# Attention kernel on one core: the key matmuls of the pair after next moved behind the second scores

## What is computed

```
q = rmsnorm(layernorm(x) @ Wq, gq)      # per head, D = 128, 16 heads
k = rmsnorm(ctx @ Wk, gk);  v = ctx @ Wv
scores = einsum('bqhd,bkhd->bhqk', q, k) / sqrt(D)
x = x + (softmax(scores) @ v) @ Wo
h = square(relu(layernorm(x) @ ternary(W_fc).T))
x = x + rmsnorm(h) @ ternary(W_proj).T
```

## Time and profile before

| | |
|---|---|
| runs | 370.31, 370.45, 375.02 us; median 370.45 us |
| span of the profiled execution | 373.6 us (its own device time is not listed apart; the span is 3.15 us over the median of the runs) |
| TensorE clock granted, mean | 0.981 of full speed; 1.00 from 40 to 340 us |
| busy | PE 347.3, DVE 308.3, ACT 295.5, POOL 256.4 us |

### The profile page before, as it was taken

How to read it: one execution, slowest core, us unless ns; L and a number is a source line. 1 busy time by engine, 2 the same in 40 slices (tenths; PEclk the granted TensorE clock), 3 DMA queues, 4 the chain that set the end, 5 groups by cost and what they waited for, 6 DMA issues and landing times.

```text
span 373.6 us, 9069 instructions
## 1 busy us (share of the span) xinstructions
PE 347.3 (93%) x2720; PEld 330.7 (89%) x2720; DVE 308.3 (83%) x697; ACT 295.5 (79%) x810; POOL 256.4 (69%) x386
## 2 busy tenths in 40 slices
PE   6778999999999999999999999999999999888975
PEld 5768999999999999999999999999999998767865
DVE  2797788888888888888888898888888986799991
ACT  3447888888888888888888888888888888777750
POOL 3653777777777787777777877777778773065761
PEclk9989999999999999999999999999999999999995
DMA  6980111111111111111111111111111100000012
GB/s 212 366 281 6 55 42 42 42 42 42 44 44 42 42 42 45 42 42 44 42 44 43 42 43 42 44 42 44 45 51 53 51 1 0 2 0 2 0 38 75
DMA packets 20341, 20.72 MB, mean 55 GB/s; under 512 B 1504, under 2 KB 19936, under 8 KB 20192
## 3 DMA queue, kind: packets, MB, share of 16 engines
q1 hardware_dynamic: 20032, 20.45, 16.9%
q10 hardware_dynamic: 288, 0.00, 0.0%
HBM read 19.40 MB, written 1.05 MB: 55 GB/s over the span
## 4 chain that ended last, share of the span: by engine, by line
PE 48%; DVE 17%; POOL 13%; issue 12%; DMA 4%; ACT 3%; POOLq 1%; SPq 0%; DVEq 0%; ACTq 0%
POOL fq L297 7%; PE bY L547 6%; DVE WWl L869 4%; PE bT L585 4%; PE bY L549 4%; PE bY L548 4%; PE bA L547 3%; PE bA L548 3%; PE bA L549 3%; PE bT L595 3%; POOL Wkh L274 3%; DVE Ol L869 3%; DMA Wkr<-in_L_xattn_Wk 3%; PE bO L547 2%; PE bO L549 2%
## 5 line engine op out<-in xcount | busy, mean ns | idle before, releaser
L416 ACT ACTIVATE Pr<-bS,nb,fq 128x256 f32<-128x256 f32 x128 | 70.9, 564 | 1.7 <-DVE nb L918 1.7
L411 ACT ACTIVATE Oh<-bO 128x256 fp32r<-128x256 f32 x64 | 24.6, 385 | 29.5 <-PE bO L549 29.1
L277 POOL TENSOR_TENSOR Wql<-Wqr,Wqh 128x512 fp32r<-128x512 f32 x32 | 41.4, 1293 | 5.9 <-POOL Wqh L274 5.9
L914 DVE TENSOR_REDUCE mx<-bS 128x2 f32<-128x512 f32 x64 | 43.8, 684 | 1.0 <-PE bS L549 0.6
L547 PE MATMUL bY<-WWh,Oh 128*128 (+1 forms) x128 | 39.1, 305 | 5.8 <-DVE Ol L869 4.9
L869 DVE TENSOR_TENSOR PTl<-bT,PTh 128x512 fp32r<-128x512 f32 x64 | 43.5, 681 | 0.9 <-ACT PTh L403 0.5
L547 PE MATMUL bS<-kh,qh 128*128 128x256 f32 x128 | 41.5, 324 | 0.6 <-DVE kl L900 0.6
L869 DVE TENSOR_TENSOR ql<-bA,qh 128x512 fp32r<-128x512 f32 x32 | 22.1, 691 | 22.1 <-ACT qh L399 22.1
L403 ACT ACTIVATE PTh<-bT 128x512 fp32r<-128x512 f32 x64 | 38.0, 594 | 1.6
L585 PE MATMUL bT<-ident,Pr 128*128 128x128 f32 x256 | 38.4, 273 | 0.4 <-ACT Pr L424 0.4
L297 POOL TENSOR_TENSOR fq<-qv,mhalf 128x4 f32<-128x4 f32 x32 | 32.5, 1014 | 7.3 <-DVE qv L910 6.9
(11 more groups left out here) (172 smaller groups left out, 1293.0 us busy)
## 6 DMA issues: line engine op xcount, KB each, us to landing
Wqr<-in_L_xattn_Wq SPq DMA_DIRECT2D x32, 256.0 KB, 2.5
Wkr<-in_L_xattn_Wk SPq DMA_DIRECT2D x32, 128.0 KB, 2.4
Wor<-in_L_xattn_Wo SPq DMA_DIRECT2D x2, 1024.0 KB, 9.6
Wvr<-in_L_xattn_Wv SPq DMA_DIRECT2D x1, 1024.0 KB, 9.6
fpr<-in_L_ffn_W_fc SPq DMA_DIRECT2D x1, 1024.0 KB, 11.2
fpr<-in_L_ffn_W_proj SPq DMA_DIRECT2D x1, 1024.0 KB, 12.8
out<-xn SPq DMA_DIRECT2D x4, 256.0 KB, 2.2
xt<-in_x SPq DMA_DIRECT2D x1, 768.0 KB, 7.5
```

The costliest lines, as they stand in the source:

```text
L277: gp.tensor_tensor(lo, src, hi.bitcast(f32), ALU.subtract).then_inc(done, 1)
L411: act.activation(Oh[u][:, :], bO[:, u * SQ:(u + 1) * SQ], ACT.Copy).then_inc(oh_done, 1)
L416: last = act.activation(Pr[u][:, t, :], bS[u][:, t * SKV:(t + 1) * SKV], ACT.Exp, bias=nb[u][:, t:t + 1], scale=fq[:, QT * u + t:QT * u + ...
L914: dve.tensor_reduce(mx[u][:, :], bS[u][:, :].rearrange("p (t k) -> p t k", t=QT), AX.X, ALU.max).then_inc(mx_done[u], 1)
```

## The change

In PE's `body`, `keys(i + 2)` stands behind `scores(i + 1, 1)` and ahead of `project(i, 0)`; it stood behind `turn_p(i, 0)`. ACT's `k_square(i + 2)` moves behind `exps(i + 1, 0)`, DVE's `var_k(i + 2)` behind `recip(i + 1, 0)`. On POOL, `split_k(i + 3)` moves from the head of the body to the place behind `rsqrt_k(i + 2)`, and `rsqrt_k(i + 2)` itself moves behind `norm_p(i + 1)`. No instruction is added or taken away, and all waits keep their semaphores and counts.

```diff
             def body(i, ln=None):                      # POOL
-                if not known(i) or i + 3 < STEPS:
-                    split_k(i + 3)
                 if not known(i) or i + 1 < STEPS:
                     rsqrt_q(i + 1)
                 if not known(i) or i + 2 < STEPS:
                     split_q(i + 2)
-                    rsqrt_k(i + 2)
                 if not known(i) or i + 1 < STEPS:
                     norm_p(i + 1)
+                if not known(i) or i + 2 < STEPS:
+                    rsqrt_k(i + 2)
+                if not known(i) or i + 3 < STEPS:
+                    split_k(i + 3)
                 ternary(i)
...
                 pt_hi(i, 0)                            # ACT
-                if not known(i) or i + 2 < STEPS:
-                    k_square(i + 2)
                 norm_p(i)
...
                     exps(i + 1, 0)
+                if not known(i) or i + 2 < STEPS:
+                    k_square(i + 2)
...
                 turn_p(i, 0)                           # PE
-                if not known(i) or i + 2 < STEPS:
-                    keys(i + 2, bm)
...
                     scores(i + 1, 1)
+                if not known(i) or i + 2 < STEPS:
+                    keys(i + 2, bm)
...
                     var_q(i + 1)                       # DVE
-                if further:
-                    var_k(i + 2)
...
                     recip(i + 1, 0)
+                if further:
+                    var_k(i + 2)
                 compare_t(i)
```

## The result

The changed kernel took a median of **411.72 us** (409.48 to 414.16, 4 runs), against 372.45 us before (370.31 to 375.02, 4 runs): ratio **1.107**, 95% interval 1.099 to 1.116. The forecast was 397.8, between 383 and 406: the right sign and the right place, but the loss is 39.3 us where 27.4 were forecast, and the time lies above the range.

The account below looks back on a forecast made before the run. PE, nearly full at 9.07 us a step, was to give way to the keys' closed loop of 9.99: 30 x 0.92 = 27.6 us of span, by 0.992 27.4, added to 370.45 gives 397.8 us, range 383 to 406.

Parts of the forecast that it names:

- The mechanism: Keys' chain, from first scores to first scores, closes each step: 9.6 to 10.2 us, 385 to 404 us; chance 0.77.
- Rivals 2 and 3: PE waits for queries' low part, 9.13 us a step, chance 0.09; or PE reaches its floor, 360 us, 0.04.
- Rival 4: DVE's kn held until POOL's Wkh ends: 10.40 us a step, 410 us; chance 0.07.
- +0.92 us a step: Growth of a step from 9.07 us to the 9.99 us of the keys' closed loop.
- 9.99: Walked length in us of the loop from one pair's first scores to the next pair's.
- my 4.25: Start of the second reciprocal on DVE, in us after the step's first scores.
- `norm_p` lasts 0.94: `kv` at 5.56: On POOL, norm_p starts at 4.62 us after first scores and lasts 0.94, so kv starts at 5.56.
- up to 0.5 "if not": Extra DVE work in layer-norm steps: taken as 0, otherwise up to 0.5 us in some 9 steps.
- 0.2 to 0.4 us a step: All that could be had if POOL's norm_p cost nothing on the loop, since the key sum ends at 5.2.
- I take the same share, 0.992: Conversion from span to time: 370.45 / 373.6, the runs' median over the profiled span, kept for the changed kernel.

Follow-up runs that it names:

- experiment 1: Changed kernel with the keys' power (rsqrt_k) again ahead of norm_p on POOL, keys still late: 391.81 us, ratio 1.050.
- experiment 7: Changed kernel with the power of the key sums computed twice, the first result unread: 464.59 us, ratio 1.240.
- experiments 4 and 5: Changed kernel with compare_t moved on DVE: behind the second o_lo, 411.74 us, ratio 1.102; or behind norm_k, 434.52 us, ratio 1.156.
- experiment 2: Changed kernel with only the key matmuls put back early on PE, all followers late: 414.69 us, ratio 1.109.
- experiments 3 and 5: First: kernel before with rsqrt_q ahead of split_k on POOL, 389.65 us, ratio 1.042. Second: changed kernel with compare_t behind norm_k, 434.52 us.

## Why the prediction was wrong

**Right, and shown.** The mechanism: the loop through reciprocal, `norm_p`, power, `kn`, `turn_k`, `kl`. It is the chain of waits in the trace, experiment 1 breaks it where the order on POOL makes it, and in experiment 7 a microsecond put in comes out as a microsecond in the steps at full clock. What the profile would show was there too: no wait ahead of the first projection, none for the split of Wk, new waits at `kn`, `turn_k`, `kl` and `rs`. `rk` starts 86.75 - 80.59 = 6.16 us after the first scores, where I had said 5.6 to 6.0, and PE waits 0.86 us for `kn`, where I had said 0.5. Rivals 2 and 3 are out. Rival 4, `kn` held, is out as well: `kn` takes 0.68 to 0.69 us in all its cases, beside `Wkh` too. That its 410 us are closer to 411.72 than my 397.8 is chance.

**The term that was too small: +0.92 us a step.** Measured it is 36.9 / 30 = 1.23 us. The 9.3 us between (36.9 for 27.6) are, from the trace and rounded:

- 0.21 us in an ordinary step (10.20 for 9.99), 6.3 us in all. Link by link, in the step shown: the reciprocal comes 0.11 us later than my 4.25 (84.95 - 80.59); `gsr`, ahead of it, now starts 0.18 us after `nb` (84.85 - 84.67) and before 0.09, and why isn't shown. `norm_p` to `kv` takes 1.17 us and not 0.94. `rk` to `kn` and `kn` to `turn_k` are 0.07 and 0.09 shorter than I had them. The step that failed is "`norm_p` lasts 0.94: `kv` at 5.56". 0.14 of its 0.23 us are `norm_p` itself, 1.08 us: that row has POOL beside `Ol` and `kn`, each with one input in PSUM; in the new order `norm_p` runs beside `compare_t`, and experiments 4 and 5 show that this is why. The other 0.09 is the gap from one POOL instruction to the next, for which I had put nothing, though rows 7 show it (`rk` ends at 198.48, `Pr` begins at 198.57); it is there in experiment 5 as well, 1.02 us from `norm_p` to `kv`. Weighing the page on the shared interface, I asked only whether it would slow `kn`, the instruction that I had moved in my mind, and didn't go through the other pairs that would newly meet.
- 1.4 us in the first interval, 11.56: TensorE's clock was at half there (below). In experiment 2's trace, where it stayed at full in that interval, it took 10.31.
- 1.7 us in three steps of 10.77, where `xn` stands between `kn` and `ql`. I had taken 0 for the layer norm and up to 0.5 "if not"; it was 0.57 in three steps.

The prediction also said that 0.2 to 0.4 us a step is all that could be had back if `norm_p` cost nothing on the loop. Experiment 1 gave 0.53: the sum of the keys ends as worked out, 5.1 us after the first scores, but what it was compared with, `kv` at 5.56, was too early (5.88 measured).

**The base.** 411.72 - 397.8 = 13.9 us. Of these 7.9 are in the span, 409.1 for the 401.2 of the prediction: 9.3 in the 30 intervals, less 1.4 outside them. The other 6.0 come from the step from span to time, "I take the same share, 0.992". It put the time 3.4 us below the span, because the only span at hand, 373.6, was set against the median of other executions, 370.45. In every execution for which both are on record the time is 2.07 to 3.64 us over the span, in the profiled one after 2.2 (411.27 for 409.1), and the median of the four lies 0.4 above that. So the profiled execution before took some 376 us, more than any of its kernel's four runs, and later medians of that kernel are 372.45 to 375.52. Neither part alone would have carried 397.8 over 406.

**The range** was drawn from the same walk with smaller links. It had 0.2 us a step of slack upwards (0.1 of it for instructions not seen) and 0.4 downwards, and none for the base, though each thing that a walk leaves out (a pause, a contention, a clock) makes it longer.

## What to carry to other kernels

When instructions are reordered, follow the moved one's successors to the same point one round later: a chain that wasn't closed, because a producer ran ahead of an unrelated wait, becomes a loop when it is put behind that wait, and then the engine with the most idle time (here POOL, 64% busy) can set the pace. Look at each engine's order for what is pushed back, as carefully as for what is brought forward: two of the misses here (experiments 3 and 5) came from that. And take a duration from the row that has the same neighbour on the other engine, not just the same instruction.

## What the runs showed of the hardware

Contention between POOL and DVE goes both ways and is large for small instructions. DVE's `nb` takes 0.16 or 0.52 us and `wneg` 0.28 or 0.82; POOL's `kv` takes 0.19 or 0.32, and one half of `norm_p` 0.48 or 0.62. In each long case DVE's instruction has both inputs in SBUF, POOL is at work, and the longer one is the one that started second: `nb` 0.11 us after `Wqh`, `wneg` 0.16 after `Wkl` in experiment 5, `kv` 0.02 after `wpos` in experiment 4, and the half of `norm_p` 0.16 after `wpos` in the changed kernel. Not every such meeting costs: the power `rk` takes 1.02 us beside `compare_t` in the kernel before, with `wneg` at 0.28, the second `nb` takes 0.16 beside `kv`, and `wneg` 0.28 beside `norm_p` in the changed kernel. The Trainium skill states such a contention (page "GPSIMD Engine Reference", section 8, Key points); these are its sizes here, with the cases that cost nothing.

TensorE's granted clock fell to its lower level of 1.2 GHz in the middle of the steps. In experiment 7 that was after idle stretches of 1.9 us in each of two steps (1.89 and 1.90 ahead of `turn_k`, and 0.34 ahead of the first scores). In the changed kernel it happened once among the steps, in step 0 (columns as above; 0.50 from 40 to 42 us):

```profile
38.00:50.00 12.00, 10.96 (x80) 10.67 (x79) 7.55 (x20) 8.26 (x26) 7.11 (x11) 0.86 0.10 31
50.00:110.00 60.00, 52.84 (x438) 51.19 (x438) 43.25 (x107) 45.67 (x137) 42.33 (x65) 1.00 0.13 38
```

From 50 to 350 us, with two waits of 0.3 to 0.9 us a step, it stayed at the full 2.4 GHz. The Trainium skill says that the clock is set by how busy PE has been (page "TensorE: Matmul & The Clock Gate", section "What's actually happening"); the traces agree in that the kernel of experiment 7, where PE waits longest for `kn`, has the lowest mean clock, 0.925. Why it fell there in about every other step and not in each, and once at 305 us in experiment 1 and not in the steps around it, no run here shows.
